# A post-layer-norm transformer block on one core: an early look moved in front of the weighted sum, and two loads reordered

## The chip, the cores and the metric

The kernel runs on one core of a Trainium2 chip. Its engines work side by side and are tied together by semaphores only: TensorE (PE, matrix products; PEld is its loading of weights), VectorE (DVE), ScalarE (ACT), GpSimd (POOL) and SyncE (SP, which here issues transfers only). The metric is the device time of one execution in microseconds (us). Before the change the median of 3 runs is 2308.47 us (2308.45 to 2308.74).

## The reference

Eight sequences of 1024 tokens with 256 features go through attention with a learned relative position, a layer norm, a feed-forward layer with binarized weights, and a second layer norm:

```python
qkv = x @ in_proj_weight.T + in_proj_bias            # 16 heads of 16
scores = einsum('bhid,bhjd->bhij', qh / 4, kh)        # 1024 x 1024 per head
bias   = (qh / 4) @ rel_pe.T, read at clip(j - i, -64, 64) + 64
attn   = softmax(scores + bias) @ vh
x = layernorm(x + attn @ out_w.T + out_b)
h = gelu(x @ binarize(w1).T + b1)                     # 1024 hidden, exact gelu
x = layernorm(x + h @ binarize(w2).T + b2)
```

The softmax is the exact one: the largest score of every row is subtracted. All of it is float32.

## The kernel before, in words

The program has three phases, each in a block of its own with an instruction stream written out by hand for every engine. The order of the work is that of the code; semaphores hold an instruction back until what it needs is there.

**Phase 1** projects the input to queries, keys and values, writes them to DRAM and prepares the weights.

**Phase 2** is the attention. It handles two heads (h = 0 and 1) at a time: 64 such steps, G = 64, each with 8 pairs m, and each pair with two units u = 2m and 2m+1, which are called its first and second half (`part` 0 and 1). The two heads lie in rows 0 to 63 and 64 to 127 of TensorE's array, so a product of one head and a product of the other can be in the array together. The engines do this in a pair:

- A *look* (line 1164, tile `ring_ps`) is a product of 128 queries with 512 keys, one for each head; it serves only to find the row maxima of a later step (24 units ahead). VectorE reads the two looks of a first half in one reduction (line 1068), and the two looks of a second half one by one, adding the band of position terms as it reads (line 1079). `ring_ps` has three slots, so a look has to wait until VectorE has read what was in its slot.
- *Weigh* (line 1203) computes the scores of the current step into `weigh_ps`; before it, *turn_bands* (line 1188) transposes the parts of the band that fall into this unit into the same bank. ScalarE takes the exponential (line 1025, tile `probs`).
- *Band product* (line 1153) computes the position terms of a step three ahead, ScalarE copies them out (lines 1012 and 1014, tile `carried`), SyncE writes them to DRAM (line 807), and GpSimd reads them back skewed by one element per row (lines 888 and 901, tile `band_all`), which is what lines the terms up with the keys.
- The *weighted sum* (line 1220, `sum_ps`) multiplies the exponentials of the pair before last with the values. It uses the array in four column groups of 32.

In `pair` on TensorE the order is: bands of the first half, look, weigh, weigh, look, band product, weighted sum (`lagging`), bands of the second half, look, weigh, weigh, look. In `products` the first look and the first weigh belong to different heads, and so do the second weigh and the second look:

```python
if looked:
    look(i, n, first)
if step >= 0:
    weigh(step, m, part, 1 - first)
    weigh(step, m, part, first)
if looked:
    look(i, n, 1 - first)
```

Steps -3 to -1 of the phase have looks and band products only. At the head of the phase SyncE waits for five constants set by GpSimd (`s_set`, 5), writes ones into two rows of the keys (line 840), and only then begins to write bands.

**Phase 3** is projection, layer norms and feed-forward layer in 16 iterations `it` of 512 tokens. For iteration 2 and on, SyncE loads the attention output (`load_heads`, line 150), the residual (`load_residual`, line 153) and the inverse softmax sums, spread over the rows of their heads (`spread_inverse`, line 165). GpSimd multiplies heads and inverse (`divide`, line 1378), adds a bias to the residual (`residual`, line 1386) and to the normalized rows (`skip`, line 1392); TensorE projects what `divide` has made (line 1546). Each waits in the order of its own engine's stream.

## Time and profile before

| | |
|---|---|
| median of 3 runs | 2308.47 us |
| the profiled execution | 2306.05 us, of which the span is 2304.1 us |
| PE busy | 2213.8 us, 96% |
| DVE busy | 1740.0 us, 76% |
| ACT busy | 1566.1 us, 68% |
| POOL busy | 1086.9 us, 47% |
| mean granted TensorE clock | 0.982 |

A row of the timeline gives the start from the beginning of the span, the duration, the engine, the line, the operation with its tiles (what is written <- what is read), a count, and in brackets how long the engine had been idle before it and what ended that. Busy is the share of time in which an engine has an instruction in it; products follow each other in TensorE like in a pipe, so that a product is listed as busy for longer than it keeps the next one out. What one of them costs is read from the distance between starts.

### The profile page before, as it was taken

The page shows a single profiled execution, that of the slowest core. Times are in us where ns is not written, and L with a number is a line of the kernel's source. Part 1 is how long each engine was busy: PE and PEld are TensorE (multiplying, and loading weights), DVE is VectorE, ACT ScalarE, POOL GpSimd, SP SyncE. Part 2 cuts the span into 40 slices and gives each one's busy share as a digit, 9 for nine tenths or more (in the row PEclk, how much of TensorE's full clock was granted, in tenths as well). Part 3 has the DMA queues.
Part 4 walks back from the last instruction along what each step waited for, and adds up shares of the span by engine and source line. Part 5 has one row for each costly group of instructions (what it writes and reads, how often), then busy time and mean ns, then how long its engine had stood idle before and what let it go on. Part 6 is the DMA issues. An engine that isn't in the chain of part 4 may idle for free. (4 is left out here: it accounts for less than half of the span.)

```text
span 2304.1 us, 47825 instructions
## 1 busy us (share of the span) xinstructions
PE 2213.8 (96%) x14580; PEld 1261.2 (55%) x14580; DVE 1740.0 (76%) x3447; ACT 1566.1 (68%) x2192; POOL 1086.9 (47%) x1803
## 2 busy tenths in 40 slices
PE   8997799999999999999999999999999999899997
PEld 5554355545555555555555555555555544788886
DVE  3444688888888888888888888888888884788885
ACT  3444277777777777777777777777777776577676
POOL 1000444555445554455554555545555442577763
PEclk9998599999999999999999999999999999999999
DMA  9997877777777777777777777777777771433321
GB/s 305 402 334 273 215 215 212 219 210 212 218 213 221 207 215 219 211 218 207 215 220 211 220 206 215 220 213 216 208 215 218 215 214 49 122 100 109 108 66 46
DMA packets 334570, 468.55 MB, mean 203 GB/s; under 512 B 89797, under 2 KB 262550, under 8 KB 334486
## 3 DMA queue, kind: packets, MB, share of 16 engines
q0 software_dynamic: 120960, 215.78, 34.6%
q1 hardware_dynamic: 204358, 243.32, 33.0%
q10 hardware_dynamic: 9168, 8.52, 1.1%
q8 instruction: 29, 0.48, 0.1%
q14 instruction: 55, 0.45, 0.1%
HBM read 244.73 MB, written 221.25 MB: 202 GB/s over the span
## 5 line engine op out<-in xcount | busy, mean ns | idle before, releaser
L1025 ACT ACTIVATE probs<-weigh_ps 128x1024 f32<-128x1024 f32 x1024 | 1047.7, 1023 | 197.3 <-PE weigh_ps L1203 188.6
L1164 PE MATMUL ring_ps<-keys,queries 48*128 48x512 f32 x2048 | 853.8, 478 | 22.0 <-DVE partial_max L1068 13.7
L1079 DVE CUSTOM_DVE_ANT_1 ring_ps<-ring_ps,band_all 128x512 f32<-128x512 f32 x1008 | 681.2, 715 | 213.6 <-PE ring_ps L1164 213.4
L1203 PE MATMUL weigh_ps<-queries,keys 50*128 50x512 f32 (+3 forms) x2688 | 748.1, 383 | 0.0
L1068 DVE TENSOR_REDUCE partial_max<-ring_ps 128x2 f32<-128x1024 f32 x512 | 627.7, 1226 | 116.2 <-PE ring_ps L1164 88.5
L1164 PEld LDWEIGHTS ring_ps<-keys,queries 48*128 48x128 f32 x2048 | 369.9, 187 | 511.7 <-issue 371.8
L1220 PE MATMUL sum_ps<-probs,values 128*32 128x512 f32 x4096 | 546.4, 605 | 0.1
L1014 ACT ACTIVATE carried<-weigh_ps 128x260 f32<-128x260 f32 (+1 forms) x512 | 211.9, 414 | 255.4 <-PE weigh_ps L1153 255.4
L925 POOL COPY carried<-carried 128x252 f32<-128x252 f32 x430 | 159.1, 395 | 458.1 <-ACT carried L1014 458.1
L1188 PE MATMUL weigh_ps<-ident,band_all 128*128 128x128 f32 x2048 | 362.5, 289 | 1.5 <-ACT carried L1014 0.6
L1203 PEld LDWEIGHTS weigh_ps<-queries,keys 50*128 50x128 f32 x2688 | 357.6, 186 | 10.4 <-issue 5.9
L1188 PEld LDWEIGHTS weigh_ps<-ident,band_all 128*128 128x128 f32 x2048 | 213.6, 141 | 225.9 <-issue 103.9
L888 POOL DMA_DIRECT2D band_all<-band_scr x320 | 227.3, 714 | 52.8 <-DMA band_scr<-carried 42.8
L1442 DVE TENSOR_TENSOR hidden<-gelu,hidden 128x512 fp32r<-128x512 f32 x128 | 143.5, 1133 | 66.8 <-ACT hidden L1504 65.5
L1153 PE MATMUL weigh_ps<-rel_terms,queries 48*128 48x130 f32 (+1 forms) x1024 | 160.4, 279 | 6.5 <-PEq L221 4.7
L1568 PE MATMUL hid_ps<-queries,sign1T 128*128 128x512 f32 x512 | 143.4, 403 | 16.9 <-ACT hidden L1504 13.0
L1502 ACT ACTIVATE gelu<-hid_ps,b_col,alpha 128x512 f32<-128x512 f32 x128 | 99.6, 778 | 76.5 <-PE hid_ps L1568 57.3
L1582 PE MATMUL out_ps<-sign2T,hidden 128*128 128x256 f32 x1024 | 149.9, 290 | 0.6 <-ACT hidden L1504 0.6
L1079 DVE DVE_READ_ACCUMULATOR2_ANT partial_max<- 128x1 f32 x1024 | 145.6, 142 | 0.0
L1582 PEld LDWEIGHTS out_ps<-sign2T,hidden 128*128 128x128 f32 x1024 | 137.9, 190 | 9.6 <-ACT hidden L1504 0.8
L1153 PEld LDWEIGHTS weigh_ps<-rel_terms,queries 48*128 48x128 f32 x1024 | 108.5, 189 | 37.7 <-ACT probs L1025 20.0
L606 PE MATMUL bank<-xT,wT 128*128 128x512 f32 x256 | 115.2, 603 | 9.9 <-ACT xT L401 9.9
(131 smaller groups left out, 1852.9 us busy)
## 6 DMA issues: line engine op xcount, KB each, us to landing
band_scr<-carried SPq DMA_DIRECT2D x256, 512.0 KB, 6.0
band_all<-band_scr POOLq DMA_DIRECT2D x128, 512.0 KB, 5.4
band_all<-band_scr POOLq DMA_DIRECT2D x128, 256.0 KB, 4.5
keys<-k_scr POOLq DMA_DIRECT2D x128, 240.0 KB, 8.1
k_scr<-k_parts SPq DMA_DIRECT2D x16, 1792.0 KB, 9.8
queries<-q_scr POOLq DMA_DIRECT2D x128, 128.0 KB, 3.8
o_scr<-weighted_s SPq DMA_DIRECT2D x64, 256.0 KB, 8.2
keys<-k_scr POOLq DMA_DIRECT2D x128, 120.0 KB, 5.2
```

Of the source, the lines that this page charges most:

```text
L888: pool.dma_start(band[:, c % SLOTS, m, :, e, c0:c1], flat(band_scr, band_base(c, m) + e * P * BAND_ROW + offset, [[BAND_ROW - 1, P], [2 * ...
L925: last = nc.gpsimd.tensor_copy(out[:, :, e, NARROW:2 * P], flat(end, 0, [end.ap[0], end.ap[1], [0, P - 2]]))
L1014: nc.scalar.activation(kept[:, :, 0:width], product[:, :, 0:width], ACT.Copy).then_inc(s_be, 1)
L1025: nc.scalar.activation(probs[:, u % PROBS], weigh_ps[weigh_of["scores", at]][:], ACT.Exp).then_inc(s_pr, 1)
L1068: nc.vector.reduce_max(partial_max[:, g, :, e, 0], ring_ps[:, first:second + 1], AX_X).then_inc(s_seen, HG)
L1079: nc.vector.tensor_tensor_reduce(out=both, in0=both, in1=bias, scale=1.0, scalar=LOWEST, op0=ALU.add, op1=ALU.max, accum_out=partial_max[: ...
L1153: last = nc.tensor.matmul(product, query_rows(c, h, ROWS, tile * P, (tile + 1) * P), moving, start=True, stop=True, tile_position=(h * ROW ...
L1164: nc.tensor.matmul(dst, query_rows(c, h, ROWS, tile * P, (tile + 1) * P), key_rows(c, h, ROWS, c0, c0 + 512), start=True, stop=True, tile_ ...
L1188: nc.tensor.matmul(weigh_ps[weigh_of["scores", at]][:, h, e * P:(e + 1) * P], band[:, c % SLOTS, tile // 2, h, tile % 2, side * P:(side + ...
L1203: last = nc.tensor.matmul(weigh_ps[weigh_of["scores", at]][:, h, e0 * P:e1 * P], key_rows(c, h, QROWS, k0, k0 + P), query_rows(c, h, QROWS ...
L1220: last = nc.tensor.matmul(sum_ps[r0:r0 + 32, :], values[:, c % SLOTS, v0:v0 + 32], probs[:, (2 * n + g) % PROBS, h], start=(n == 0), stop= ...
L1582: last = nc.tensor.matmul(out_ps[:, t], hidden[:, it % 2, c, j, t * P:(t + 1) * P], sign2T[:, j], start=(c == 0 and j == 0), stop=(c == 1 ...
```

## The change

It has three parts.

1. On TensorE the first look of a pair's second half is issued right behind the pair's band product and before the weighted sum (`pair`); `products` then issues only the other look of that half, behind the two weighs.
2. On SyncE the ones for the keys are written after the first four chunks of bands, in step -2, and no longer at the head of phase 2.
3. At the start of phase 3 SyncE issues the spread inverse of iterations 2 and 3 ahead of their heads and residual, and GpSimd does `skip(0)` before `divide(2)`, and `divide(3)` before `skip(1)`.

```diff
@@ sync, attention
-                sp.wait_ge(s_set, 5)
-                for h in range(HG):
-                    row = keys[h * ROW_TILE + ROWS:h * ROW_TILE + QROWS].bitcast(F32)
-                    sp.dma_start(flat(row, 0, [row.ap[0], [P, SLOTS * KCOLS // P], [1, P]]),
-                                 flat(ones[:], 0, [ones[:].ap[0], [0, SLOTS * KCOLS // P], [1, P]])
-                                 ).then_inc(s_one, 16)
                 for step in range(-START, FIRST):
                     for u in range(UNITS):
+                        if step == 1 - START and u == NT:
+                            sp.wait_ge(s_set, 5)
+                            for h in range(HG):
+                                row = keys[h * ROW_TILE + ROWS:h * ROW_TILE + QROWS].bitcast(F32)
+                                sp.dma_start(flat(row, 0, [row.ap[0], [P, SLOTS * KCOLS // P], [1, P]]),
+                                             flat(ones[:], 0, [ones[:].ap[0], [0, SLOTS * KCOLS // P], [1, P]])
+                                             ).then_inc(s_one, 16)
                         unit(0, step, u)
@@ tensor, products
-                    if looked:
+                    if looked and part == 0:
                         look(i, n, first)
@@ tensor, pair
                     if bands_at(step, m):
                         band_product(i, band_index(step, m))
+                    if looks_at(step, 2 * m + 1):
+                        second = look_index(step, 2 * m + 1)
+                        look(i, second, look_heads[second][0])
                     lagging(i, step, m)
@@ sync, feed-forward
-                    if it >= 2 * EARLY:
+                    if it < 2 * EARLY:
+                        spread_inverse(sp, it, inverse_wide)
+                    else:
                         load_sums(sp, it)
                     load_heads(sp, it, heads_raw)
                     load_residual(sp, it, x_in)
                     if it >= 2 * EARLY:
                         write_inverse(sp, it)
-                    spread_inverse(sp, it, inverse_wide)
+                        spread_inverse(sp, it, inverse_wide)
@@ gpsimd, feed-forward
+                skip(0)
                 divide(2)
                 residual(2)
-                skip(0)
+                divide(3)
+                skip(1)
                 for it in range(IT + 2):
...
-                    if it + 1 < IT:
+                    if 0 < it and it + 1 < IT:
                         skip(it + 1)
-                    if it + 3 < IT:
+                    if 0 < it and it + 3 < IT:
                         divide(it + 3)
```

On TensorE, in step 0 of the attention (L1153 is the band product, L1220 the weighted sum, L1164 a look, L1203 a weigh, L1188 a band transpose), a pair reads so before:

```order
199 L1153 MATMUL weigh_ps<-rel_terms,queries 128x130 x2
200 L1220 MATMUL sum_ps<-probs,values 32x512 x4
201 L1131 REGISTER_ALU
202 L1125 REGISTER_ALU
203 L1164 MATMUL ring_ps<-keys,queries 128x512
204 L1203 MATMUL weigh_ps<-queries,keys 128x512 x2
205 L1125 REGISTER_ALU
206 L1164 MATMUL ring_ps<-keys,queries 128x512
207 L1129 REGISTER_ALU
208 L1188 MATMUL weigh_ps<-ident,band_all 128x128 x4
```

and the same pair after the change (its lines have moved by one):

```order
199 L1154 MATMUL weigh_ps<-rel_terms,queries 128x130 x2
200 L1126 REGISTER_ALU
201 L1165 MATMUL ring_ps<-keys,queries 128x512
202 L1221 MATMUL sum_ps<-probs,values 32x512 x4
203 L1132 REGISTER_ALU
204 L1204 MATMUL weigh_ps<-queries,keys 128x512 x2
205 L1126 REGISTER_ALU
206 L1165 MATMUL ring_ps<-keys,queries 128x512
207 L1130 REGISTER_ALU
208 L1189 MATMUL weigh_ps<-ident,band_all 128x128 x4
```

One look has moved over the weighted sum; it now stands beside no product of the other head, and the two weighs stand beside each other.

On SyncE at the head of the attention, before:

```order
50 L798 UNCONDITIONAL_BRANCH
51 L840 DMA keys<-ones 2x60x128 x2
52 L807 DMA band_scr<-carried 128x4x256 x8
53 L817 DMA queries<-minus_max 2x8x128 x2
54 L807 DMA band_scr<-carried 128x4x256 x4
```

and after:

```order
50 L798 UNCONDITIONAL_BRANCH
51 L807 DMA band_scr<-carried 128x4x256 x4
52 L843 DMA keys<-ones 2x60x128 x2
53 L807 DMA band_scr<-carried 128x4x256 x4
54 L817 DMA queries<-minus_max 2x8x128 x2
```

Four writes of bands now come before the ones.

On GpSimd at the start of phase 3 (L1378 is `divide`, L1386 `residual`, L1392 `skip`), before:

```order
288 L1378 TENSOR_TENSOR carried<-heads_raw,inverse_wide 128x1024
289 L1386 TENSOR_TENSOR carried<-x_in,bo_row 128x1024
290 L1392 TENSOR_TENSOR x_b<-x_even,b_row 128x1024
291 L1392 TENSOR_TENSOR x_b<-x_odd,b_row 128x1024
292 L1378 TENSOR_TENSOR carried<-heads_raw,inverse_wide 128x1024
293 L1386 TENSOR_TENSOR carried<-x_in,bo_row 128x1024
```

and after (L1384 is `divide`, L1392 `residual`, L1398 `skip`):

```order
288 L1398 TENSOR_TENSOR x_b<-x_even,b_row 128x1024
289 L1384 TENSOR_TENSOR carried<-heads_raw,inverse_wide 128x1024
290 L1392 TENSOR_TENSOR carried<-x_in,bo_row 128x1024
291 L1384 TENSOR_TENSOR carried<-heads_raw,inverse_wide 128x1024
292 L1398 TENSOR_TENSOR x_b<-x_odd,b_row 128x1024
293 L1392 TENSOR_TENSOR carried<-x_in,bo_row 128x1024
```

The second `divide` has moved over both `skip`s.

## Rows read from the trace of the kernel before

**Rows 1.** Waits, 400 to 1800 us: waiting engine and line <- releaser: us, times, longest.

```profile
PEld ring_ps L1164 <- DVE partial_max L1079: 22.5, 110, 0.8
PEld ring_ps L1164 <- DVE partial_max L1068: 18.5, 105, 0.5
PEld weigh_ps L1153 <- ACT probs L1025: 17.4, 108, 0.2
```

**Rows 2.** Timeline of PE, a pair in which the last look waits.

```profile
1011.23 0.28 PE L1203 MATMUL weigh_ps<-queries,keys 50*128 50x256 f32 x1
1011.35 0.22 PE L1153 MATMUL weigh_ps<-rel_terms,queries 48*128 48x130 f32 x2
1011.50 1.07 PE L1220 MATMUL sum_ps<-probs,values 128*32 128x512 f32 x8
1012.50 0.49 PE L1164 MATMUL ring_ps<-keys,queries 48*128 48x512 f32 x1
...
1013.37 0.44 PE L1188 MATMUL weigh_ps<-ident,band_all 128*128 128x128 f32 x2
```

**Rows 3.** Timeline of PE, the next pair: no look waits.

```profile
1014.34 0.33 PE L1153 MATMUL weigh_ps<-rel_terms,queries 48*128 48x130 f32 x2
1014.60 1.07 PE L1220 MATMUL sum_ps<-probs,values 128*32 128x512 f32 x8
...
1015.97 0.50 PE L1164 MATMUL ring_ps<-keys,queries 48*128 48x512 f32 x1
...
1016.31 0.39 PE L1164 MATMUL ring_ps<-keys,queries 48*128 48x512 f32 x1
1016.63 0.66 PE L1188 MATMUL weigh_ps<-ident,band_all 128*128 128x128 f32 x4
```

**Rows 4.** Timeline of PE, the last of the eight pairs from 1005.13 us on.

```profile
1028.47 0.44 PE L1188 MATMUL weigh_ps<-ident,band_all 128*128 128x128 f32 x2
1029.61 0.28 PE L1171 MATMUL ring_ps<-ident,negative_parts 128*32 128x128 f32 x1
```

**Rows 5.** Timeline of ACT, SP and DVE, head of the attention.

```profile
220.88 0.41 ACT L1014 ACTIVATE carried<-weigh_ps 128x260 f32<-128x260 f32 x1
224.05 1.48 SPq L840 DMA_DIRECT2D keys<-ones  x2
225.58 6.91 SPq L807 DMA_DIRECT2D band_scr<-carried  x4
233.42 0.38 ACT L1012 ACTIVATE carried<-weigh_ps 128x252 f32<-128x252 f32 x1 [8.40 <-DMA band_scr<-carried]
239.73 1.23 DVE L1068 TENSOR_REDUCE partial_max<-ring_ps 128x2 f32<-128x1024 f32 x1 [20.47 <-DMA band_all<-band_scr]
```

**Rows 6.** DMA issues of the page: count, KB each, us to landing.

```profile
band_scr<-carried SPq DMA_DIRECT2D x256, 512.0 KB, 6.0
```

**Rows 7.** Timeline of SP and POOL, start of phase 3.

```profile
1961.07 1.35 SPq L150 DMA_DIRECT2D heads_raw<-o_scr  x2
1973.34 2.34 POOL L1378 TENSOR_TENSOR carried<-heads_raw,inverse_wide 128x1024 f32<-128x1024 f32 x1 [28.89 <-DMA inverse_wide<-inverse_scr]
1978.39 2.80 POOL L1392 TENSOR_TENSOR x_b<-x_even,b_row 128x1024 f32<-128x1024 f32 x1
1983.51 2.35 POOL L1378 TENSOR_TENSOR carried<-heads_raw,inverse_wide 128x1024 f32<-128x1024 f32 x1
```

**Rows 8.** The chain that ended last: the transfer of iteration 3's inverse.

```profile
1967.64 10.79 DMA inverse_wide<-inverse_scr
```

**Rows 9.** Timeline of PE, start of phase 3.

```profile
1975.73 5.41 PE L1546 MATMUL att_ps<-woT,carried 128*128 128x256 f32 x16 [3.38 <-POOL carried L1378]
1985.91 1.25 PE L1546 MATMUL att_ps<-woT,carried 128*128 128x256 f32 x4 [1.98 <-POOL carried L1378]
```

**Rows 10.** Windows: busy us of each engine, PEclk, DMA share, GB/s.

```profile
400.00:1800.00 1400.00, 1396.20 (x9986) 708.64 (x9982) 1132.64 (x2241) 1032.89 (x1388) 714.59 (x1389) 1.00 0.75 214
1976.00:1979.00 3.00, 3.00 (x10) 2.36 (x10) 2.98 (x2) 0.00 (x0) 3.00 (x2) 0.59 0.41 147
```

## The prediction

> **What bounds the kernel now.** I read the windows first. From 400 to 1800 us TensorE has an instruction in it for 1396.20 of 1400 us, at the full clock, while VectorE has 1132.64 and ScalarE 1032.89 [rows 10]. So in the attention the path runs over TensorE, and what counts there is its distances between starts and the short waits that a busy share of 99.7% hides. The waits of that stretch show them: the loading of a look's weights is held up 110 and 105 times by VectorE's reads of `ring_ps`, that of a band product 108 times by the exponential [rows 1]. The timeline then tells what a wait costs a pair. In one pair the block behind the weighted sum (look beside weigh, weigh beside look) takes from 1012.50 to 1013.37, 0.87 us [rows 2]; in the next, where no look waits, from 1015.97 to 1016.63, 0.66 us [rows 3]. The difference, 0.21, is TensorE waiting for the slot of the last look and then loading weights with nothing beside it. Two other stretches are bound by transfers: VectorE's first look at 239.73 [rows 5], and TensorE's two waits for `divide` at the start of phase 3, 3.38 and 1.98 us [rows 9].
>
> **Part 1, the look ahead of the sum: what it adds.** It concerns each second half that looks: steps 0 to 61 with 8 pairs and step 62 with 4, together 500 pairs. No instruction is added, and TensorE changes its way of dividing the array as often as before. What changes is the company. Before, the first look of the half (1012.50, 1015.97) runs beside a weigh of the other head. After, the two weighs run beside each other and the second look alone, so the block is as long as before, 0.66. The moved look stands alone between band product and sum and is paid for in full. From a block without waits: the first 512 columns take 0.34 from start to start (1015.97 to 1016.31), of which some 0.12 is the load of the weights (the step from one small product to the next on the same rows: 1011.23 to 1011.35), so 0.22 is the streaming; and from the last look to the next kind of product it is 0.32 (1016.31 to 1016.63) [rows 2, 3]. Band product to sum takes 0.15 (1011.35 to 1011.50). With the look between them it is 0.12 for its load, since that begins when the band product on the same rows has taken its own, and 0.32 from it to the sum: 0.44, that is +0.29 a pair. If its load hides altogether, +0.22. The trace has no look alone in this place; these two are my bounds, and I take 0.29, because every step of small products on the same rows shows the 0.12. 500 x 0.29 = +145 us.
>
> The Trainium skill, "TensorE: Matmul & The Clock Gate", section "Back-to-back issue gap", gives about 216 ns for an isolated product of 512 columns and about 131 ns in a sustained stream. By the first the sum would stay near my lower bound, by the second the moved look would cost 0.13 x 500 = 65 us and the kernel would come out faster. The trace shows 0.22 for the streaming of one on its rows, with the first figure.
>
> **Part 1: what it removes.** VectorE gets the look of the second half about a microsecond earlier, so it need not idle between its reduction and the next read, and the last look's slot is free by the time that TensorE has finished a later sum and the weighs. The time from the start of the sum to the next band transpose (or, at the end, to the turn of the maxima, 1028.47 to 1029.61 [rows 4], less 0.37 for two transposes before it, as from 1014.60 + 1.00 to 1015.97 in rows 3) is 1.66 without waits (1.00 + 0.66). The eight pairs from 1005.13 on take 0.17, 0.19, 0.21, 0, 0.07, 0.15, 0.15 and 0.11 more, the third and fourth of them being those of rows 2 and 3: 1.05 us, 0.13 a pair. I let all of it go: the sum starts 0.29 later and the slot is free earlier, not later. The second thing is the band product's wait for the exponential: 1014.34 to 1014.60 is 0.26 where 0.15 is usual [rows 3], 0.11 for the load laid bare. Both weighs now end in the first of the two places of the block, so the exponential starts about 0.2 earlier against what follows. 108 of some 428 pairs have such a wait [rows 1], in others the load is partly bare; where two transposes stand between, as in rows 3, it stays, since there the exponential's 1.02 us is just too long. I take 0.09 a pair for this and for the waits at the turned maxima, with 0 and 0.12 as bounds. Removed: 0.13 + 0.09 = 0.22 a pair, 500 x 0.22 = -110 us.
>
> Part 1 together: +0.07 a pair, **+35 us**. With its bounds: 0.22 - 0.25 = -0.03, -15 us; 0.29 - 0.13 = +0.16, +80 us. The new wait that comes with it: the moved look needs the slot of the pair before's last look, and behind it in TensorE's queue stands the sum. VectorE reads that slot last before its next reduction, which it starts 0.1 to 0.3 before the look is due; I add nothing.
>
> **Part 2, the ones behind four band writes.** The first chunk is copied at 220.88 + 0.41 = 221.29, but SyncE issues its write at 225.58, behind the ones (224.05, 1.48 us of issuing, itself behind GpSimd's constants); it has landed when ScalarE goes on at 233.42, after 7.8 us, where 6.0 is the median of such a write [rows 5, 6]. Issued at 221.3 it lands between 227.3 and 229.1, 4.3 to 6.1 us earlier. What follows (the read back, VectorE's first reduction at 239.73 after 20.47 us idle for `band_all`) is a chain without slack, and the steps -3 to -1 behind it go at VectorE's pace, so the start of step 0 moves with it. **-5 us**, between -3 (another transfer, the keys, ends last) and -6.5. The ones are needed only in step 0, and their issuing falls into ScalarE's wait for the first chunk; if that cover were gone it would cost their 1.5 us.
>
> The Trainium skill, "DMA: Bandwidth & Descriptors", section on why a DMA increments its semaphore by 16, says that a copy runs on as many engines as divide its slowest dimension, at most 16; the ones, with two rows, would then sit on two engines, and a band write that uses all has to queue there. The 7.8 against 6.0 us fit that. By it the write after would take 6.0 us and this part would be -6.1.
>
> **Part 3, the start of phase 3.** Heads, residual and inverse of iterations 2 and 3 are six loads of 512 KB, issued from 1961.07 on. The third, iteration 2's inverse, is in at 1973.34, and the sixth at 1967.64 + 10.79 = 1978.43 [rows 7, 8]. With the inverse first, `divide(2)` waits for two of three: 12.3 x 2/3 = 8.2 us, 1969.3; it ends at 1971.6, and TensorE, free from 1975.73 - 3.38 = 1972.35, no longer waits [rows 9]. `divide(3)` is at 1983.51 behind two skips, although its data were there at 1978.43; after, it waits for five loads of six, 17.4 x 5/6 = 14.5 us, 1975.6, at the latest 1978.4, and ends 2.35 later. TensorE's own work from 1975.73 to its second wait is 8.2 us, part of it at 0.59 of the clock after the 3.38 us idle [rows 10]; without that idle about 7, which puts the product of 1985.91 at 1979.4. **-6.5 us**, between -5 and -8.5. Late next is GpSimd's `skip(1)` and `residual(3)`, about as late as TensorE.
>
> **Sum.** 35 - 5 - 6.5 = +23.5 us on the profiled execution's 2306.05 gives 2329.5. It lies 2.4 below the median of the runs, so I add the same to the median: 2308.5 + 23.5 = **2332 us**.
>
> **The rivals.**
> A, *the last look alone is the whole price, and every wait goes* (the other side). The moved look's load hides under the band product, so it costs 0.22, and the waits for the exponential and for the maxima go too: 0.13 + 0.10. That is -0.01 a pair, -5 us, and 2308.5 - 5 - 11.5 = 2292. For it: PE's loads often start beside a product. Against it: they do so only after the product before has started, and 0.12 is what that leaves. It is decided at +0.014 a pair, below which parts 2 and 3 make the kernel faster by over 0.2%. Chance 0.25.
> B, *half and half*: 0.25 for the look, 0.23 removed, +0.02 a pair, +10 us, with -11.5 comes out at 2307, no change. Chance 0.13.
> C, *the waits don't go*: the moved look meets its own wait for the slot and holds up the sum, so that of 0.22 only the 0.13 is recovered: +0.16 a pair, +80 us, 2377. Against it is VectorE's idle time, which the earlier look removes. With half of that, +55 us, 2352. Chance 0.17.
> D, *parts 2 and 3 give nothing*, because the keys end last in the one and GpSimd's later work in the other: 2308.5 + 35 = 2344. Chance 0.08, inside the range.
> The forecast itself, 2318 to 2345, has 0.37.
>
> About 0.2% (4.6 us) is what a measurement of this kernel can tell from no change. Faster 0.25 (A), same 0.13 (B), slower 0.62 (forecast, C, D). The range for 8 in 10 reaches from the middle of A to the milder form of C: 2293 to 2354.
>
> **What would show it.** In the steady part: band product to sum 0.44 in place of 0.15, with a look between; sum to transposes 1.66 in nearly every pair; no wait of a look for VectorE in the block behind the sum; a period of eight pairs longer by about 0.55 us. At the head: the first band write issued near 221.3, VectorE's first reduction near 235, the ones in front of the fifth write. In phase 3: `divide(2)` near 1969 and `divide(3)` near 1977 as counted from the block's start at 1961, TensorE without the 3.38 us. I am wrong if band product to sum comes out at 0.37 or less, or if the blocks of the first half shrink by more than 0.12 a pair.

## The result and the profile after

| | before | after |
|---|---|---|
| median of the runs | 2308.6 us (4 runs) | 2351.9 us (2350.1 to 2353.4, 4 runs) |
| the profiled execution | 2306.05, span 2304.1 | 2351.03, span 2349.3 |
| PE, DVE, ACT busy | 96%, 76%, 68% | 97%, 74%, 67% |
| mean granted clock | 0.982 | 0.982 |

The changed kernel is slower by 43.3 us, ratio 1.0187 (1.0172 to 1.0203; in brackets behind a ratio stands its 95% interval). The forecast was +23.5, so the sign was right, and +43.3 lies in the range (2293 to 2354), 2 us inside its upper end. The span grew by 45.2 us; read from one landmark to the next it is made up so:

| stretch | after - before, us |
|---|---|
| phase 1 (first band product 0.71 earlier, untouched by the change) | -0.7 |
| head of the attention, to the first transpose of step 0 | -2.3 |
| step 0, to its turn of the maxima | +1.0 |
| the next 61 steps, 488 pairs, to the turn of step 61 | +50.5, 0.103 a pair |
| the rest of the attention | +0.5 |
| start of phase 3, to the transposes of iteration 4 | -5.2 |
| iteration 9 of phase 3 | +1.5 |
| the rest | -0.1 |

**A pair.** Two pairs of the timeline of TensorE after the change, to be laid beside [rows 2, 3] (line 1165 is a look, 1204 a weigh, 1154 the band product, 1221 the weighted sum, 1189 a band transpose):

```profile
1011.12 0.23 PE L1154 MATMUL weigh_ps<-rel_terms,queries 48*128 48x130 f32 x2
1011.18 0.45 PE L1165 MATMUL ring_ps<-keys,queries 48*128 48x512 f32 x1
1011.55 1.07 PE L1221 MATMUL sum_ps<-probs,values 128*32 128x512 f32 x8
1012.55 0.50 PE L1204 MATMUL weigh_ps<-queries,keys 50*128 50x512 f32 x2
1012.89 0.39 PE L1165 MATMUL ring_ps<-keys,queries 48*128 48x512 f32 x1
1013.21 0.66 PE L1189 MATMUL weigh_ps<-ident,band_all 128*128 128x128 f32 x4
...
1014.42 0.22 PE L1154 MATMUL weigh_ps<-rel_terms,queries 48*128 48x130 f32 x2
1014.49 0.44 PE L1165 MATMUL ring_ps<-keys,queries 48*128 48x512 f32 x1
1014.86 1.07 PE L1221 MATMUL sum_ps<-probs,values 128*32 128x512 f32 x8
1015.86 0.50 PE L1204 MATMUL weigh_ps<-queries,keys 50*128 50x512 f32 x2
```

Band product to sum is 0.43 and 0.44, where 0.44 was forecast for 0.15; sum to transposes is 1.66. Behind the sum only one of the half's two looks is left, and the block of weighs and look is still 0.66 long: the look that left it took no time with it.

The waits from 400 to 1800 us (columns as in [rows 1]):

```profile
PEld weigh_ps L1154 <- ACT probs L1026: 16.0, 52, 0.3
PEld ring_ps L1165 <- DVE partial_max L1080: 0.7, 3, 0.3
PEld ring_ps L1165 <- DVE partial_max L1069: 0.6, 2, 0.3
```

The 41 us of waits of looks for VectorE have become 1.3. The band product's wait for the exponential has gone from 108 times to 52, but from 17.4 us only to 16.0. Sorted by the pair of the period of eight in which they stand, 53 waits of one pair (8.5 us) and four others are gone, and the 51 of the pair before it (8.3 us) have become 52 that take 16.0, twice as long each.

The windows, to be laid beside [rows 10]:

```profile
400.00:1800.00 1400.00, 1399.79 (x9682) 685.68 (x9678) 1102.63 (x2175) 1007.00 (x1347) 695.35 (x1350) 1.00 0.74 208
2010.00:2013.00 3.00, 3.00 (x8) 2.11 (x8) 0.00 (x0) 2.74 (x4) 2.35 (x1) 0.57 0.28 91
```

**The distances by block.** These come from the starts of TensorE's instructions, medians over the periods of eight pairs (one step) from 400 to 1850 us, summed over a period. "Before the sum" is the stretch from a pair's first look to its sum; "behind the sum" begins where the sum (0.996 us everywhere) and any transposes right behind it have ended, and lasts to the next transposes.

| kernel | period | before the sum | behind the sum |
|---|---|---|---|
| before | 26.20 | 6.72 | 6.37 |
| after | 27.03 | 8.72 | 5.27 |

The block behind the sum lost 1.10 us of 8 pairs, 0.137 a pair. The one before it gained 2.00. In four pairs of the period it grew by 0.280 to 0.286, in the other four by less; if the moved look costs 0.284 everywhere, the other four gave back 8 x 0.284 - 2.00 = 0.27, 0.034 a pair. Nearly half of that (0.128) is the one pair whose waits for the exponential went. The stretch at the turn gave 0.009.

**The head.** ScalarE, SyncE and DVE, to be laid beside [rows 5]:

```profile
220.18 0.41 ACT L1015 ACTIVATE carried<-weigh_ps 128x260 f32<-128x260 f32 x1
220.61 4.09 SPq L807 DMA_DIRECT2D band_scr<-carried  x4
224.75 2.42 SPq L843 DMA_DIRECT2D keys<-ones  x2
236.69 1.23 DVE L1069 TENSOR_REDUCE partial_max<-ring_ps 128x2 f32<-128x1024 f32 x1 [18.14 <-DMA band_all<-band_scr]
```

The first write goes out at once, 5 us earlier, but VectorE starts only 3.0 earlier, 2.3 after the head start from phase 1. From 218 to 235 us the DMA view gives, in us to landing, before

```profile
band_scr<-carried SPq DMA_DIRECT2D x4, 512.0 KB, 7.1
keys<-k_scr POOLq DMA_DIRECT2D x2, 240.0 KB, 5.5
```

and after

```profile
band_scr<-carried SPq DMA_DIRECT2D x4, 512.0 KB, 9.8
keys<-k_scr POOLq DMA_DIRECT2D x2, 240.0 KB, 6.6
```

The marks with which a transfer counts its sixteen parts as landed tell more. Before, fourteen parts of the first write were in by 230.94 us and the last two at 233.28 and 233.34, 1.4 us behind the last mark of the ones (231.95); the keys' loads had ended at 229.59. After the change fourteen parts were in by 224.29, 3.7 us after the issue, and the last two at 229.83 and 229.86. Of the 64 marks of the keys' loads 56 were in by 224.54, and the last eight came from 228.44 to 230.82. Part 2 alone shows the same (223.77, then 228.96 and 228.98). So two parts of the write were late in both kernels: before, right behind the ones; after, while the last parts of the keys' loads were under way. No run took the keys away, so that it is they that hold the two parts is read from these times and not shown by an experiment.

**Phase 3.** The block starts at 2009.9 us. GpSimd and TensorE, beside [rows 7, 9] (1398 is `skip`, 1384 `divide`, 1554 the projection):

```profile
2009.97 2.37 POOL L1398 TENSOR_TENSOR x_b<-x_even,b_row 128x1024 f32<-128x1024 f32 x1 [16.56 <-POOLq L628]
2020.53 2.37 POOL L1384 TENSOR_TENSOR carried<-heads_raw,inverse_wide 128x1024 f32<-128x1024 f32 x1 [8.18 <-DMA heads_raw<-o_scr]
2027.45 2.40 POOL L1384 TENSOR_TENSOR carried<-heads_raw,inverse_wide 128x1024 f32<-128x1024 f32 x1 [1.79 <-DMA heads_raw<-o_scr]
```

```profile
2022.95 3.72 PE L1554 MATMUL att_ps<-woT,carried 128*128 128x256 f32 x16 [0.96 <-POOL carried L1384]
2029.91 1.13 PE L1554 MATMUL att_ps<-woT,carried 128*128 128x256 f32 x4 [0.41 <-POOL carried L1384]
```

`divide(2)` is 10.6 us behind the start of the block; before it was 12.4, and the forecast said 8.3. It now waits for the heads: the first two of an iteration's three loads are not in after two thirds of the time, since those issued behind them are under way together with them; that this is the cause is read from the order of the landings only. `divide(3)` is 17.5 us behind the start, where the forecast had 16. TensorE's waits of 3.38 and 1.98 us are down to 0.96 and 0.41 all the same, and iteration 2 is 6.5 us earlier against the end of the attention, as forecast. Of these, iterations 2 and 3 give back 1.3 (19.7 and 21.3 us where they were 19.2 and 20.5).

### The profile page after: what moved, and what is told of

Its sections match the earlier page's. It is cut to its first block and busy times, and to the rows that moved or that the text cites. A ratio compares the mean times of both kernels' runs of the same rounds, so it can differ in the third digit from the quotient of the medians.

```text
span 2349.3 us, 47812 instructions
## 1 busy us (share of the span) xinstructions
PE 2269.5 (97%) x14580; PEld 1257.7 (54%) x14580; DVE 1745.8 (74%) x3447; ACT 1572.9 (67%) x2192; POOL 1088.6 (46%) x1803
## 3 DMA queue, kind: packets, MB, share of 16 engines
q0 software_dynamic: 120960, 215.78, 34.7%
## 5 line engine op out<-in xcount | busy, mean ns | idle before, releaser
L1165 PE MATMUL ring_ps<-keys,queries 48*128 48x512 f32 x2048 | 803.0, 443 | 18.9 <-DVE partial_max L1069 9.5
L1080 DVE CUSTOM_DVE_ANT_1 ring_ps<-ring_ps,band_all 128x512 f32<-128x512 f32 x1008 | 700.0, 695 | 141.0 <-PE ring_ps L1165 135.4
L1204 PE MATMUL weigh_ps<-queries,keys 50*128 50x512 f32 (+3 forms) x2688 | 635.1, 403 | 0.0
L1204 PEld LDWEIGHTS weigh_ps<-queries,keys 50*128 50x128 f32 x2688 | 304.5, 185 | 346.0 <-ACT carried L1015 305.6
L1154 PE MATMUL weigh_ps<-rel_terms,queries 48*128 48x130 f32 (+1 forms) x1024 | 153.7, 266 | 5.9 <-PEq L221 4.7
L1221 PEld LDWEIGHTS sum_ps<-probs,values 128*32 128x32 f32 x4096 | 80.9, 108 | 125.4 <-issue 123.4
```

The source lines that it names most:

```text
L1080: nc.vector.tensor_tensor_reduce(out=both, in0=both, in1=bias, scale=1.0, scalar=LOWEST, op0=ALU.add, op1=ALU.max, accum_out=partial_max[: ...
L1154: last = nc.tensor.matmul(product, query_rows(c, h, ROWS, tile * P, (tile + 1) * P), moving, start=True, stop=True, tile_position=(h * ROW ...
L1165: nc.tensor.matmul(dst, query_rows(c, h, ROWS, tile * P, (tile + 1) * P), key_rows(c, h, ROWS, c0, c0 + 512), start=True, stop=True, tile_ ...
L1204: last = nc.tensor.matmul(weigh_ps[weigh_of["scores", at]][:, h, e0 * P:e1 * P], key_rows(c, h, QROWS, k0, k0 + P), query_rows(c, h, QROWS ...
L1221: last = nc.tensor.matmul(sum_ps[r0:r0 + 32, :], values[:, c % SLOTS, v0:v0 + 32], probs[:, (2 * n + g) % PROBS, h], start=(n == 0), stop= ...
```

## The experiments

All ratios are to the kernel before. Twelve further kernels ran.

**The parts by themselves.** The edit of the first is the two hunks on TensorE alone; of the second, the hunks on SyncE and GpSimd alone; of the third, the first hunk of SyncE; of the fourth, the two hunks of phase 3.

> Part 1 alone on the kernel before. Theory (the look stands alone and costs 0.284 us a pair, 0.137 of waits in the block behind the sum go, 0.034 of waits of the band product and 0.009 at the turned maxima go, net +0.104 a pair, 500 pairs): +52 us, ratio 1.0225; no gain at the head or in phase 3. Rival (part of the +45 us comes out of parts 2 and 3, which push the pairs or the feed-forward iterations into a worse rhythm): +45 us or less, ratio below 1.020, and the period of eight pairs below 27.0 us.

Measured: 1.0241 (1.0227 to 1.0255), +55.6 us. Part 1 carries the whole loss, and a little over. Its period is 27.02 us, the changed kernel's 27.03. Of the 56.2 us by which its span is longer, 50.3 lie in the 61 steps and 2.8 in step 0, where moved looks alone would make 0.8. There TensorE, which is granted half of the full clock in the steps before, in which it waits, gets the full one 19 us after the step's start; in the changed kernel it is 15 and before it was 12. That differs between kernels whose step 0 is the same, too: part 3 alone, which changes nothing there, took 2.2 us more for step 0 than the kernel before. The windows of part 1 alone (the number before the last two is the granted clock):

```profile
285.00:288.00 3.00, 3.00 (x16) 1.00 (x13) 1.89 (x3) 1.30 (x2) 0.37 (x1) 0.50 1.10 184
291.00:294.00 3.00, 3.00 (x18) 0.90 (x15) 1.89 (x3) 1.51 (x2) 0.40 (x1) 0.50 0.75 229
```

and of the changed kernel:

```profile
285.00:288.00 3.00, 3.00 (x20) 1.92 (x24) 0.96 (x3) 1.21 (x2) 0.00 (x0) 0.72 0.79 232
```

> Parts 2 and 3 without the moved look. Theory: the head gives 2.3 us, the start of phase 3 gives 6.5 us of which about 2.8 are lost again in later iterations: -6 us, ratio 0.9974. Rival 1 (the forecast's own terms, 5 and 6.5): -11.5 us, ratio 0.9950. Rival 2 (the 2.8 us lost later are an accident of the changed kernel and not of part 3): -8.8 us, ratio 0.9962. The last two are told apart in the trace, by the distance of the second iteration's transposes and the last one's.

Measured: 0.9966 (0.9953 to 0.9979), -7.8 us, nearest to the second rival's 0.9962, with the theory's 0.9974 inside the interval and the first rival's 0.9950 outside. In its trace VectorE begins 3.9 us earlier (1.0 of it from phase 1), and iteration 2 another 6.8, of which 1.3 come back. The long iteration 9 is there too, but it is no loss: see below.

> Part 2 alone: the ones behind four band writes. Theory: the first write goes out 5 us earlier but takes 9.4 us in place of 7.8 because it is under way together with the keys, and what ends last after it is its read back; step 0 starts 2.3 to 3.0 us earlier, ratio 0.9989. Rival (the forecast's term): -5 us, ratio 0.9978. Second rival: no part of it survives, since step 0 waits for something else, ratio 1.000.

Measured: 0.9993 (0.9985 to 1.0002), 1.6 us faster and not told from no change; the rival's 0.9978 is outside the interval. Its profiled execution has VectorE begin 4.9 us earlier, 3.6 without phase 1. All nine profiled kernels of this study that have part 2 give 2.3 to 3.6 for it, 3.1 in the mean, counted from the first band product; the four others lie within 0.15 of the kernel before. None reaches the forecast's 5.

> Part 3 alone. Theory: at the second iteration's transposes it is 6.5 us ahead of the kernel before, gives 1.3 us back over the next two iterations, which come out 19.7 and 21.3 us long in place of 19.2 and 20.5, and keeps 5.2: ratio 0.9977. Rival 1 (the forecast's 6.5 all stay): 0.9972, and no longer iteration. Rival 2 (what matters is the TensorE clock, which TensorE's idle time at the start of the phase lowers at some executions and not at others): between 0 and -8 us from execution to execution, with the granted clock below 1 in a stretch where before had it at 1.

Measured: 0.9971 (0.9962 to 0.9981), -6.7 us. Iteration 2 comes 6.6 us earlier, and the next two are 19.7 and 21.3 us long: 5.3 stay in the trace, and the median allows for both theory and first rival. The clock has a share in it: the dip of [rows 10] at 1976 us is away, and one at the start of the block is new (0.50 from 1961 to 1964 us, where before it was 1.00); the transposes of iteration 1 come 0.8 us later for it. The windows of this run:

```profile
1961.00:1964.00 3.00, 2.53 (x6) 2.10 (x7) 0.00 (x0) 1.93 (x3) 2.38 (x1) 0.50 0.19 64
1976.00:1979.00 3.00, 3.00 (x17) 2.62 (x16) 2.97 (x3) 0.34 (x1) 0.78 (x2) 1.00 0.55 170
```

**Iteration 9 of phase 3** takes 22.6 us in the changed kernel and in all the experiments, phase 3 touched or not, and 21.1 in the profiled execution of before alone. There GpSimd's `divide` found its load late (the last mark of its spread inverse came at 2140.56 us, 7.9 us after the issue, where it took 5.3 after the change), and VectorE's work beside it went faster. VectorE, before and then after:

```profile
2136.00 4.08 DVE L1442 TENSOR_TENSOR hidden<-gelu,hidden 128x512 fp32r<-128x512 f32 x3
```

```profile
2179.77 6.26 DVE L1450 TENSOR_TENSOR hidden<-gelu,hidden 128x512 fp32r<-128x512 f32 x3
```

GpSimd, before and then after:

```profile
2140.68 2.40 POOL L1378 TENSOR_TENSOR carried<-heads_raw,inverse_wide 128x1024 f32<-128x1024 f32 x1 [1.76 <-issue]
```

```profile
2182.64 2.84 POOL L1384 TENSOR_TENSOR carried<-heads_raw,inverse_wide 128x1024 f32<-128x1024 f32 x1
```

So 1.5 of the 45.2 us of span are luck of one execution. The medians differ by 43.3, which fits that, though the other executions of the kernel before have no profile to show it.

**What a lone look costs.** In the changed kernel, the moved look was made narrower, which leaves out part of the row maxima:

```diff
-                        look(i, second, look_heads[second][0])
+                        look(i, second, look_heads[second][0], 256 if step >= 0 else 512)
```

and then the same with 32.

> The changed kernel with the moved look cut from 512 to 256 columns in all pairs from step 0 on (the row maxima of half of a look are left out, so the output differs). Theory (of the 0.29 that the moved look adds between band product and sum, 0.22 is the streaming of its 512 columns at 0.42 ns each, all of it on the path): 0.107 us a pair less, band product to sum 0.33 in place of 0.44, -53 us against the changed kernel, ratio to before 0.996. Rival 1 (the price is that of one more product of any width, loading and emptying the array): no change, ratio 1.019. Rival 2 (a shorter look bares another limit, VectorE or the exponential): less than 30 us come back, ratio above 1.006.

> The changed kernel with the moved look cut to 32 columns from step 0 on (most of that look's row maxima are left out). Theory: streaming falls from 0.22 to 0.013, what stays of the moved look is the load of its weights, 0.07 to 0.12 us a pair; band product to sum 0.22 to 0.27, about -98 us against the changed kernel if nothing else ends last, ratio to before 0.976. Rival 1: fixed price, ratio 1.019. Rival 2 (TensorE gets so much faster that it waits for the exponential or for VectorE's slots again): the gain over the half-width look is under 25 us, ratio 0.985 or more, and waits return before band product and looks.

Measured: 0.9984 (0.9972 to 0.9996) with 256 columns and 0.9925 (0.9909 to 0.9941) with 32. TensorE with 256, and then with 32:

```profile
1009.23 0.22 PE L1154 MATMUL weigh_ps<-rel_terms,queries 48*128 48x130 f32 x2
1009.29 0.33 PE L1165 MATMUL ring_ps<-keys,queries 48*128 48x256 f32 x1
1009.55 1.06 PE L1221 MATMUL sum_ps<-probs,values 128*32 128x512 f32 x8
```

```profile
1002.66 0.22 PE L1154 MATMUL weigh_ps<-rel_terms,queries 48*128 48x130 f32 x2
1002.72 0.23 PE L1165 MATMUL ring_ps<-keys,queries 48*128 48x32 f32 x1
1002.88 1.07 PE L1221 MATMUL sum_ps<-probs,values 128*32 128x512 f32 x8
```

From look to sum it is 0.37, 0.26 and 0.16 us with 512, 256 and 32 columns: 0.44 ns a column, so 0.21 of the 0.284 is streaming of the columns beyond 32. The rest is 0.06 from band product to look and little more: the 0.12 for the load that the forecast put there is hidden by half, and the streaming is what the look costs. The first experiment is as the theory said (-47 us against the changed kernel for -53). The second shows the second rival: it gained only 14 us over the first, because waits of looks for VectorE came back. The block behind the sum went from 0.66 to 0.77 us:

```profile
PEld ring_ps L1165 <- DVE partial_max L1069: 58.0, 320, 0.6
```

Its period is 26.04 us.

**Company or place.** The moved look one place earlier, on the other head's rows than the look before it (and, for that, heads, slots and VectorE's reading order alternate with the pair):

```diff
+                    if looks_at(step, 2 * m + 1):
+                        second = look_index(step, 2 * m + 1)
+                        look(i, second, look_heads[second][0])
                     if bands_at(step, m):
                         band_product(i, band_index(step, m), order)
-                    if looks_at(step, 2 * m + 1):
...
```

> The changed kernel with the moved look one place earlier: right behind the first half's last look and ahead of the band product, always on the other head's rows (except that the head that moves and its slot alternate with the pair, and the band product begins with the head whose rows are free first). The same instructions, but the moved look has a look of the other head beside it and one band product too. Theory (a product without company is paid in full, one with company for the part that sticks out over the other head's rows): the moved look then costs 0.15 to 0.2 in place of 0.284 a pair, -40 to -65 us, ratio to before 0.991 to 1.002. Rival 1 (the place before the sum is what costs, since three looks and two weighs need three streams of 512 columns on one head's rows wherever they stand): -10 us or less, ratio 1.015 to 1.019. Rival 2 (the slot isn't free yet 0.3 us earlier, and band product and sum queue behind the look): ratio above 1.02 and waits of the look for VectorE.

Measured: 1.0145 (1.0122 to 1.0169), 10 us less than the changed kernel. The block before the sum is 8.40 us a period in place of 8.72. Company was worth 0.04 to 0.05 us in four pairs of the period, not the 0.1 of the theory; the pair behind the turned maxima lost 0.21, and the other three grew by 0.01 to 0.04, with waits of looks for VectorE back (44.7 us from 400 to 1800 us, where the changed kernel had 1.3). The first rival has it, if a little outside its range of 1.015 to 1.019: the look costs nearly the same wherever it stands in front of the sum. What is then paid for, the next experiment shows from the other side. In the changed kernel the look that stayed behind the sum is cut to 32 columns (most of its row maxima are left out):

```diff
                     if looked:
-                        look(i, n, 1 - first)
+                        look(i, n, 1 - first, 32 if part == 1 and step >= 0 else 512)
```

> The changed kernel with the other look of the second half, the one behind the two weighs, cut to 32 columns from step 0 on (most of its row maxima are left out); the moved look keeps its 512. It asks why the block behind the sum did not become shorter when a look left it. Theory (a block lasts as long as the head with more 512-column streams in it: after the change that is 2 for one head and 1 for the other behind the sum, 3 and 2 before it, so one stream more in all than the 2 and 2, 2 and 2 of before): the block behind the sum falls from 0.66 to 0.44 to 0.48, the one before the sum stays at 1.01 to 1.06, unless waits of VectorE's slots come back there; about -0.2 a pair, -90 us against the changed kernel at most, ratio 0.98 to 0.99. Rival 1 (the block's length is that of its three loads and the emptying of the array, whatever streams): it stays near 0.62, ratio 1.015. Rival 2 (VectorE's pace ends last as soon as TensorE is quicker): waits of looks for VectorE come back in the block before the sum and leave a period of eight pairs of about 26.0 us.

Measured: 1.0081 (1.0061 to 1.0101), -24 us against the changed kernel. TensorE in this run:

```profile
1003.38 1.07 PE L1221 MATMUL sum_ps<-probs,values 128*32 128x512 f32 x8
1004.37 0.50 PE L1204 MATMUL weigh_ps<-queries,keys 50*128 50x512 f32 x2
1004.71 0.18 PE L1165 MATMUL ring_ps<-keys,queries 48*128 48x32 f32 x1
1004.82 0.66 PE L1189 MATMUL weigh_ps<-ident,band_all 128*128 128x128 f32 x4
```

The block falls from 0.66 to 0.45 in every pair: it had been as long as the two 512-column streams of one head, with the other head's rows idle for half of it. That is the price of the change. Call the pass of 512 columns through one head's rows a stream. Before, each head had two streams in the block before the sum and two in the block behind it. Now the head with the moved look has three before the sum and the other two, and behind it one has two and the other one. A block lasts as long as the head with more streams in it, so that the pair pays for five streams where it paid for four. The second half of the theory failed. The block before the sum took back 0.16 of the 0.21, because the exponential now ends last there:

```profile
PEld weigh_ps L1154 <- ACT probs L1026: 60.4, 169, 0.5
```

The ratio stayed far above the theory's 0.98 to 0.99. Nor was the second rival's period of 26.0 reached (26.61): not VectorE, as it had it, but ScalarE was late next.

**The exponential earlier, without a lone look.** On the kernel before, in the second half only, the order in short:

```diff
-look(first), weigh(1 - first), weigh(first), look(1 - first)
+weigh(first), weigh(1 - first), look(first), look(1 - first)
```

> On the kernel before, the second half issues weigh, weigh, look, look in place of look, weigh, weigh, look; both kinds still alternate between the two row groups, so no product is without company. It tells the price of the exponential's waits from that of the lone look. Theory (what the earlier exponential is worth is 0.034 us a pair in the block before the sum): -17 us if VectorE is not held up, ratio 0.993. Rival 1 (the forecast's 0.09 a pair): -45 us, ratio 0.980. Rival 2 (VectorE, which idles 0.44 us before such a look already, gets the first look of the half 0.3 us later and passes the delay on to the slots of ring_ps): the looks of the next pair wait up to 0.3 us more, +0.1 to +0.2 a pair, ratio 1.02 to 1.04.

Measured: 1.0154 (1.0141 to 1.0167), slower by 35 us. Theory and first rival fell. VectorE gets the half's first look 0.34 later. The price is 0.07 a pair, smaller than the second rival's 0.1 (in the same view of the kernel before these waits are 188.2, 22.5 and 18.5 us):

```profile
DVE ring_ps L1079 <- PE ring_ps L1164: 267.4, 418, 1.2
PEld ring_ps L1164 <- DVE partial_max L1079: 37.7, 145, 0.7
PEld ring_ps L1164 <- DVE partial_max L1068: 1.4, 3, 0.5
```

VectorE waits longer for the looks of the second half, but the waits of looks for VectorE are 39.1 us together, where they were 41.0. That the delay comes round through the slots, as the second rival had it, is therefore not shown; what makes up the 0.07 stays open.

What the earlier exponential gives cannot be read from this kernel either; for it there is only the difference of the traces before and after the change, 0.034.

**The slot waits removed for nothing on TensorE.** On the kernel before, VectorE reads the first half's looks one by one, and slots go round:

```diff
-                        nc.vector.reduce_max(partial_max[:, g, :, e, 0], ring_ps[:, first:second + 1],
-                                             AX_X).then_inc(s_seen, HG)
+                        for at, h in enumerate(look_heads[n]):
+                            dve.wait_ge(s_look, cnt(i, HG * UNITS, HG * n + at + 1))
+                            slot = slot_of["look", HG * n + h]
+                            nc.vector.reduce_max(partial_max[:, g, h:h + 1, e, 0], ring_ps[:, slot:slot + 1],
+                                                 AX_X).then_inc(s_seen, 1)
```

> The kernel before, but VectorE reads the two looks of a first half one by one and no longer in one reduction, and the three slots of ring_ps go round in the order of the looks, so that each look waits for the look three places earlier alone. TensorE's order is that of before. It asks what the waits that the moved look removed are worth when nothing is paid on TensorE for removing them. Theory (the 0.137 us a pair of slot waits go, VectorE pays some 0.15 us more a pair, 3.1 of 3.27 us, and still keeps up): up to -68 us, ratio 0.97 to 0.98. Rival 1 (VectorE becomes the bound: at 3.1 us busy and 0.1 or more lost between its instructions it can't go below some 3.25 a pair): within 0.5% of before. Rival 2 (the later end of the second of the two reductions holds up the looks more than the earlier end of the first helps): slower by 1% or more, waits of looks for VectorE above the 41 us of before.

> The same with parts 2 and 3 of the change, as the version that may beat both kernels. Theory: its ratio is that of the reductions read apart less 0.003 (-7 us), 0.968 to 0.977. Rivals as there: 0.992 to 1.002 where VectorE becomes the bound, above 1.007 where the looks wait longer.

> The changed kernel with the first half's two looks read one by one and the three slots going round. With the reductions read apart and no moved look the waits of the block behind the sum had gone, and others had come up in the block before it: there the no-wait length is about 0.73 us and 0.85 is usual. Does the moved look pay when it takes its 0.28 out of these? Theory (a moved look is 0.28 of streams on TensorE whoever waits, and of the 0.12 to 0.2 a pair of waits in the block before the sum it can take all at best): slower than the same kernel without the moved look by 0.08 to 0.16 a pair, ratio 1.009 to 1.026. Rival 1 (those waits are VectorE's, idle 282 of 1400 us for the looks of the second half, and the moved look feeds it earlier, so all go and the price is half hidden): within 0.4% of the kernel that reads apart with parts 2 and 3, ratio 0.988 to 0.996. Rival 2 (the slots now serialize the moved look too): ratio above 1.03.

Measured: 0.9957 (0.9941 to 0.9974) alone, 0.9915 (0.9899 to 0.9932) with parts 2 and 3, and 1.0151 (1.0127 to 1.0175) with the whole change. The theories of the first two failed, that of the third held. The block behind the sum is 0.67 in nearly every pair, as after the change. The theory had -68 us for that. But the period is 26.14 us for 26.20: the block before the sum grew by nearly what the other lost (7.60 and 5.42 us for 6.72 and 6.37). The ratio is the one that the first rival gave, but not for its reason: VectorE is busy for 1107 of 1400 us, less than before (1133), and waits 293 us of them for the looks of the second half, so it isn't the bound. The waits of the loader of weights:

```profile
PEld ring_ps L1167 <- DVE partial_max L1071: 236.9, 341, 0.8
PEld ring_ps L1167 <- DVE partial_max L1082: 39.4, 160, 0.6
PEld weigh_ps L1156 <- ACT probs L1027: 27.1, 161, 0.2
```

The first line looks like the answer and is none: 225 of its us are 268 waits of 0.84 each under the weighted sum, in which the loader has nothing to do and TensorE works; the kernel before has more of it, 320 such waits or 268 us, only without a releaser's name. The other two lines are 22.5 us, 110 times, and 17.4 us, 108 times, in the kernel before. Their growth of 26.6 us is 0.06 a pair of the 0.11 by which the block before the sum grew; the rest isn't accounted for by a wait.

Half of the -9.9 us come from the steps before step 0, where VectorE sets the pace (29.4 us for 34.7). With parts 2 and 3 it is the fastest kernel of this study, 2287.8 us where the kernel before had 2307.2. With the moved look added the period is 26.94, 0.10 a pair more than without, as in the plain kernel; the theory's 0.08 to 0.16. Of the look's 0.28 the block before the sum takes up 0.15, the rest of the pair 0.03, and the remainder is paid. In this last profile TensorE's clock also stayed at half until 312 us: step 0 took 4.4 us more than in the changed kernel, and step 1 36.7 us where 26.9 is usual, 14 us of its span together.

## Why the prediction was right in sign and short in size

- **Moved look, +0.29 a pair.** Right: 0.284, band product to sum 0.44. Its inner working wasn't: the forecast put 0.12 on the load and 0.22 on the streaming and took off what the two hide of each other; by the narrow looks it is about 0.06 and 0.22. A's hope, that the load hides altogether, was half true.
- **Waits for the last look's slot, -0.13 a pair.** Right: -0.137. C's new wait did not appear (1.3 us from 400 to 1800). Rows 1 alone would have given less: the 41 us of these waits are 0.097 a pair, since they do not hold the loads of weights laid bare behind a wait.
- **Band product's wait for the exponential and the turned maxima, -0.09 a pair.** This is the term that was mis-sized: 0.034 + 0.009 = 0.043. It was read correctly that the wait stays in pairs with two transposes, that it occurs 108 times, and that it has 0.11 in the pair of [rows 3]. But the 17.4 us of it [rows 1] are 0.04 a pair for some 428 pairs, all of them together. The other 0.05 was put on bare loads and on the turn. Blocks were read as if they had waited that are longer in themselves: after the change the block before the sum still takes 1.01 us in some pairs and 1.06 in others where no such wait is listed. And of the waits only those of one pair of the period went; where they stayed, the block grew by the whole look.
- **Part 1 together, +0.07 forecast, +0.104 measured**, 52 us for 35. Inside the bounds given, +0.16 and -0.03.
- **Part 2, -5.** Measured 3.1 in the mean. The first write left at 220.61, as forecast, but GpSimd could read it back only 9.85 us later, where it had been 8.4. What the forecast read from the Trainium skill ("DMA: Bandwidth & Descriptors", section "Why a DMA increments its semaphore by 16 and not by 1"), that the ones sit on two engines and a band write has to queue there, agrees with the trace before: two of the write's sixteen parts were late, right behind the ones. The step that failed is that the write would take the usual 6.0 us once the ones were out of its way: issued 5 us earlier, it is under way beside the keys' loads, and two parts are late again. The forecast had this only as its lower bound, -3, "another transfer, the keys, ends last", and there the measurement is.
- **Part 3, -6.5.** 6.5 at iteration 2, 5.2 from iteration 4 on. `divide(2)` came 10.6 us after the block's start and not 8.3: loads issued close together ended close together here, and a time by the number of loads didn't hold. Iteration 2 came out at 6.5 all the same, although waits of 0.96 and 0.41 us stayed that the forecast had at nothing: that the number fits is luck in part.
- **Sum.** 52 - 3 - 5.2 = +44 against the median's +43.3, with the differences of step 0 and of the clock within 3 us. That it is in the range owes something to luck: part 1 was 17 us dearer than forecast, and the range was wide enough for it. Of the rivals, the milder C had this time (2352) and half of its reason: the waits beside the 0.13 did mostly stay, but they are those of the exponential, and the new wait for the slot, which gave C its name, did not come.

## What to carry to other kernels

Where two row groups of TensorE work in parallel, count streams per row group and block, not products: here a product taken out of a balanced block freed nothing (0.66 us with it and without) and cost its whole stream where it went (0.284). Before a wait is given a price, set its row's total over the number of the places. For the exponential that gave 0.04 a pair, near the measured 0.043, where comparing blocks of different length gave 0.09. It is no strict ceiling, though: for the slots it gave 0.097, and 0.137 came back, with the loads that a wait lays bare. A loader's wait under a long product costs nothing, however large its row is. And removing a wait in one place (slots, 0.137 a pair) can bring as little as 0.007 a pair, as it did when nothing was paid for it on TensorE and the block before the sum grew instead.

## What the runs showed of the hardware

- TensorE's granted clock went from half to full 12 us after the start of step 0 in the profile of before, 15 in the changed kernel's, 19 in that of part 1 alone and 48 in that of the whole change with split reductions. The last makes 14 us of a span against the changed kernel's, and the runs of that kernel spread by 14 us (2337.4 to 2351.1). What decides the moment no run here shows. Parts worth 2 us weren't told from nothing by the median of eleven runs (part 2 alone: 0.9985 to 1.0002).
- A VectorE operation over two SBUF inputs of 512 columns takes 0.68 us alone; three of them took 6.26 in a row where GpSimd was at work on two operations beside them, and 4.08 where it was idle between the two and only the first stood beside them. The Trainium skill, "SBUF — State Buffer", section "SBUF: two separate sides", says that the two engines share one pair of ports as an exclusive lock that is held for a whole instruction; the trace agrees. It also shows an iteration that was 1.5 us shorter when a load for GpSimd was late.
- A transfer's parts can land far apart: fourteen of sixteen parts of a 512 KB write were in 3.7 us after its issue and the last two after 9.2, while loads from another queue were under way.
